# Issuing two query loads one tile ahead and splitting one read-back into three, in an offset-attention layer on eight cores

## What is computed

```
qkv = x @ qkv_w.T + qkv_b                     # q, k, v with 16 heads of 64
qs = einsum('bhnd,od->bhno', q, scale_embed)
for i, o in enumerate(OFFSETS):               # 44 offsets
    qk = einsum('bhnd,bhnd->bhn', q, shift(k, o))
    lg = qk * inv * (1.0 + qs[..., i]) + pos_bias[i]
    logits.append(where(pos >= o, lg, NEG))
p = softmax(stack(logits, -1), -1)
out = sum_i p[..., i] * shift(v, OFFSETS[i])
out = (out * if_gain) * sigmoid(x @ gate_w.T + gate_b) @ out_w.T + out_b
```

## Time and profile before

| what | us |
|---|---|
| time before, median of 2 runs | 3035.9 (3025.26 and 3046.54) |
| the profiled execution, its own time | 3036.02 |
| its span, on the slowest core (core 7) | 3033.6 |
| spans of all cores | 3019.7 to 3033.6 |
| attention, 16 tiles, in that span | 877 to 2311 |

### The profile page before, as it was taken

How to read it: one execution, slowest core, us unless ns; L and a number is a source line. 1 busy time by engine, 2 the same in 40 slices (tenths; PEclk the granted TensorE clock), 3 DMA queues, 4 the chain that set the end, 5 groups by cost and what they waited for, 6 DMA issues and landing times.

```text
span 3033.6 us, 18303 instructions; the slowest of 8 cores (3019.7 to 3033.6 us)
## 1 busy us (share of the span) xinstructions
PE 803.2 (26%) x4872; PEld 377.1 (12%) x4872; DVE 1039.1 (34%) x1142; ACT 864.1 (28%) x952; POOL 317.6 (10%) x267
## 2 busy tenths in 40 slices
PE   0139766556420111111111111111111710001620
PEld 0114322222210000000000000000000300001310
DVE  1430110000025445555454555444453043233134
ACT  1543221112123322333322333322231331003333
POOL 1000000000001011110011111011112000210000
PEclk9999998768655555555555555555555855555765
DMA  2322112223232222222222222222224032002023
GB/s 71 104 70 22 14 11 30 54 55 60 70 109 53 61 66 63 61 70 65 46 61 62 67 61 63 51 62 59 65 57 109 21 125 85 5 12 72 25 99 123
DMA packets 395686, 184.97 MB, mean 61 GB/s; under 512 B 342368, under 2 KB 353648, under 8 KB 395584
## 3 DMA queue, kind: packets, MB, share of 16 engines
q10 hardware_dynamic: 205184, 68.63, 9.8%
q1 hardware_dynamic: 147568, 82.54, 8.7%
q0 software_dynamic: 42832, 32.64, 6.2%
HBM read 111.73 MB, written 78.32 MB: 63 GB/s over the span
## 4 chain that ended last, share of the span: by engine, by line
DMA 31%; DVE 23%; ACT 16%; PE 15%; issue 7%; ACTq 5%; SPq 1%; POOL 1%; DVEq 1%; POOLq 0%
PE kqps L325 8%; DVE rbuf L538 6%; DMA rimg<-rbuf 5%; ACT rbuf L539 5%; ACTq L591 4%; DMA psp_img<-Pb 3%; DVE bandx L573 3%; DMA qtok<-qts 2%; DVE scr L570 2%; DMA accTb<-acch 2%; DMA q_img<-qtmp 2%; PE opps L754 2%; PE fps L901 2%; DMA ktok<-wcol 2%; DMA xt<-xs 2%
## 5 line engine op out<-in xcount | busy, mean ns | idle before, releaser
L523 PE MATMUL genps<-kfm,qsl 64*128 64x160 f16 (+2 forms) x768 | 92.8, 337 | 1183.6 <-DMA qtb<-qtok 691.2
L325 PE MATMUL kqps<-y1fm,wcol 128*128 128x512 f16 x1408 | 371.4, 421 | 52.5 <-ACT qtmp L367 30.3
L538 DVE CAST rbuf<-genps 128x640 f16<-128x640 f32 (+2 forms) x96 | 331.8, 3456 | 138.4 <-DMA rimg<-rbuf 111.4
L539 ACT CAST rbuf<-genps 128x640 f16<-128x640 f32 (+2 forms) x96 | 331.8, 3457 | 148.5 <-DMA psp_img<-Pb 73.2
L523 PEld LDWEIGHTS genps<-kfm,qsl 64*128 64x128 f16 x768 | 40.2, 115 | 1250.2 <-issue 1250.0
L325 PEld LDWEIGHTS kqps<-y1fm,wcol 128*128 128x128 f16 x1408 | 144.0, 106 | 235.3 <-issue 119.1
L604 ACT ACTIVATE t2b<-t2b 128x736 f32<-128x736 f32 x16 | 13.1, 816 | 547.1 <-DVE t2b L601 547.1
L664 POOL TENSOR_TENSOR acch<-vtok,Pb 128x1024 f16<-128x1024 f16 x16 | 30.3, 1892 | 1059.2 <-DMA rimg<-rbuf 800.2
L489 DVE TENSOR_TENSOR outfl<-outfl,accTb 128x128 f16<-128x128 f16 x128 | 37.6, 294 | 270.5 <-DMA psp_img<-Pb 136.1
L476 PE MATMUL pvps<-pspsb,vtok 128*64 128x128 f16 x384 | 112.2, 413 | 54.6 <-DMA band<-rimg 38.8
L358 DVE COPY vtok<-trpv 128x512 f16<-128x512 f16 x56 | 23.8, 425 | 272.5 <-PE trpv L352 272.5
(11 more groups left out here) (122 smaller groups left out, 1566.8 us busy)
## 6 DMA issues: line engine op xcount, KB each, us to landing
pspsb<-psp_img ACTq DMA_DIRECT2D x16, 1536.0 KB, 6.9
x1r<-x_img ACTq DMA_DIRECT2D x32, 512.0 KB, 3.2
xt<-xs POOLq DMA_DIRECT2D x28, 512.0 KB, 3.9
rimg<-rbuf SPq DMA_DIRECT2D x32, 416.0 KB, 2.4
rimg<-rbuf SPq DMA_DIRECT2D x32, 384.0 KB, 2.7
rimg<-rbuf SPq DMA_DIRECT2D x32, 320.0 KB, 2.2
xres<-xs ACTq DMA_DIRECT2D x16, 512.0 KB, 3.6
x_img<-x1t SPq DMA_DIRECT2D x16, 512.0 KB, 2.6
```

The lines of the kernel that those rows point to most:

```text
L325: e.matmul(_o, _s, _m, start=_st, stop=_sp),
L523: e.matmul(_o, _s, _m, start=True, stop=True, tile_position=_tp), waits, ("TS", 1))
L538: cpf = (lambda e, _o=pout, _i=pin: e.tensor_copy(_o, _i)) if eng == "vector" else \
L539: (lambda e, _o=pout, _i=pin: e.copy(_o, _i))
```

## The change

In stage A the loads of `qsl` and `pbmb` are now those of the next tile (`emit_qp_loads(qt + 1)`), with the batch name of that tile; tile 0 loads its own first. Their waits for a free buffer move with them. `qtb` is still loaded for the current tile, in a batch of its own (`"kq"`). In stage B2 the read of `psp_img` becomes three DMAs of 512 KB in one batch.

```diff
-    qsl_tok = [None, None]; pbm_tok = [None, None]
+    qsl_tok = {}; pbm_tok = {}
+
+    def emit_qp_loads(nqt):
+        if nqt >= NQT:
+            return
+        nsl = nqt % 2
+        qsl_tok[nqt] = S("scalar", lambda e, _o=qsl[nsl][:],
+                         _i=bass.AP(t["q_img"], nqt * 128, [[TOK, 128], [128 * TOK, 8], [1, 128]]):
+                         e.dma_start(out=_o, in_=_i), (last_gen.get(nqt - 2),), ("AQ", 16), batch=("ld", nqt))
+        pbm_tok[nqt] = S("scalar", lambda e, _o=pbmb[nsl][:],
+                         _i=bass.AP(t["pbm"], nqt * 128 * CW, [[CW, 128], [1, CW]]):
+                         e.dma_start(out=_o, in_=_i), (pbm_used.get(nqt - 2),), ("AQ", 16), batch=("ld", nqt))
...
     def stage_A(qt):
...
-        qsl_tok[slot] = S("scalar", lambda e, _o=qsl[slot][:],
...
-        pbm_tok[slot] = S("scalar", lambda e, _o=pbmb[slot][:],
...
+        if qt == 0:
+            emit_qp_loads(0)
+        emit_qp_loads(qt + 1)
         qtb_ev[qt] = S("scalar", lambda e, _o=qtb[:],
...
-                       (ew_lastmul.get(qt - 1),), ("AQ", 16), batch=("ld", qt))
+                       (ew_lastmul.get(qt - 1),), ("AQ", 16), batch=("kq", qt))
...
-                    waits = [qsl_tok[slot], gen_free.get((qt, genidx - 2)),
+                    waits = [qsl_tok[qt], gen_free.get((qt, genidx - 2)),
...
-               (v1, pbm_tok[slot], exp_tok.get(qt - 1)), ("VS", 1))
+               (v1, pbm_tok[qt], exp_tok.get(qt - 1)), ("VS", 1))
...
     def stage_B2(qt):
         ibase = (qt % 2) * NB * 128 * 2048
-        src = bass.AP(t["psp_img"], ibase, [[2048, 128], [128 * 2048, NB], [1, 2048]])
-        dst = bass.AP(pspsb[:].tensor, 0, [[NB * 2048, 128], [2048, NB], [1, 2048]])
-        psp_rd[qt] = S("scalar", lambda e, _o=dst, _i=src: e.dma_start(out=_o, in_=_i),
-                       (psp_wr[qt], pv_tok.get((qt - 1, 7))), ("AQ", 16), batch=("pr", qt))
+        rd = None
+        for ib in range(NB):
+            src = bass.AP(t["psp_img"], ibase + ib * 128 * 2048, [[2048, 128], [1, 2048]])
+            dst = pspsb[:, ib * 2048:(ib + 1) * 2048]
+            rd = S("scalar", lambda e, _o=dst, _i=src: e.dma_start(out=_o, in_=_i),
+                   (psp_wr[qt], pv_tok.get((qt - 1, 7))), ("AQ", 16), batch=("pr", qt))
+        psp_rd[qt] = rd
```

More of the change, by code:

```diff
@@ L494, in stage_A @@
         slot = qt % 2
-        qsl_tok[slot] = S("scalar", lambda e, _o=qsl[slot][:],
-                          _i=bass.AP(t["q_img"], qt * 128, [[TOK, 128], [128 * TOK, 8], [1, 128]]):
-                          e.dma_start(out=_o, in_=_i), (last_gen.get(qt - 2),), ("AQ", 16), batch=("ld", qt))
-        pbm_tok[slot] = S("scalar", lambda e, _o=pbmb[slot][:],
-                          _i=bass.AP(t["pbm"], qt * 128 * CW, [[CW, 128], [1, CW]]):
-                          e.dma_start(out=_o, in_=_i), (pbm_used.get(qt - 2),), ("AQ", 16), batch=("ld", qt))
+        if qt == 0:
+            emit_qp_loads(0)
+        emit_qp_loads(qt + 1)
         qtb_ev[qt] = S("scalar", lambda e, _o=qtb[:],
```

## The result

The changed kernel takes 3045.3 us (median of 29 runs) where the kernel before took 3031.3 us on the same chip (28 runs): a ratio of 1.0052, 95% interval 1.0037 to 1.0066, or 11 to 20 us more (the two medians alone are 14 us apart; here and below the interval goes with the ratio).

The account below looks back on a forecast made before the run. The prediction took each tile to be bound by the `psp_img` write of `Pb`, through the wait on SyncE's queue. Tile 0 (7.0) plus collision (5.6) added 12.6 us to 3036.0, giving 3048; range 3031 to 3062.

Parts of the forecast that it names:

- What bounds a tile: ScalarE's first copy in a tile waits for the `psp_img` write of `Pb`, 4.4 us mean; the loads have 4.1 us slack.
- The prefetch doesn't reach TensorE: Tiles 1 to 14: matmuls still wait for `qtb`, which is issued after the loads land; TensorE begins 2.6 us later.
- The cover holds, cost 0: Tiles 1 to 14: ScalarE finishes 2.6 us later, still 1.5 us before the copy released by the `psp_img` write; cost 0.
- The meeting with the write: Tiles 1 to 14: `qtb` in flight beside the large `psp_img` write delays it 0.4 us each, 5.6 us in all (0 to 13.2).
- my upper bound of 0.94: Most that `qtb` could delay the large `psp_img` write in a tile, if all of it goes first: 0.94 us.
- the mark that I had set for being wrong: The prediction counts as wrong if the large `psp_img` write takes over 5.6 us; about 5.0 was expected.
- The rule that I had left out of the sum: Engines alternate between queues, so the `psp_img` write pays for most of `qtb`: 14 x 0.8 = 11 us in place of 5.6.
- Tile 0, 7.0 us: Attention start: three loads in series without cover delay the first matmul by 7.0 us, between 5.4 and 12.3.
- The read in three, 0: Splitting the `psp_img` read into three DMAs costs 0: 13.7 us slack on ScalarE's queue, 4.5 us in tile 15.
- Rival C: Matmuls start some 4 us earlier per tile, gaining 0 in tiles 1 to 15; tile 0 pays; given 3030 us, chance 0.06.
- Rival B: First `rbuf` copy, tiles 1 to 14: cover used up, TensorE 3.8 us later; 3061 us, far end 3092; chance 0.12.
- The sum: Whole kernel: 7.0 us for tile 0 plus 5.6 for the collision of `qtb` with the write, 12.6 us slower.

Follow-up runs that it names:

- the last kernel: Changed kernel plus exact waits on SyncE's and ScalarE's queues, `qtb` in the loads' batch, stage C's matmuls waiting exactly too; against the kernel before 0.9440, 2863.5 us.

## Why the prediction was right, and where it was not

The forecast was 3048 us, 12 us over the profiled execution of before; measured were 11 to 20 us over before. Sign and size were right; the terms were less so, and that the total fits better than they do is partly luck.

- **What bounds a tile** (the write of `Pb`, by way of the wait on all of SyncE's queue): right, and shown by taking it away (0.9649), together with two other waits on the same queue. A tile became 5.9 us shorter, where ScalarE had idled 4.4 us behind the write.
- **The prefetch doesn't reach TensorE**, and `qtb` comes later: right; TensorE still waits 16 times for `qtb`. `qtb` is issued 2.7 us later (mean), as forecast, but the start slipped by 2.1 us (mean; 2.0 in the tile shown) and not 2.6, because `qtb`, issued alone, lands in 2.8 us (median) and not the 3.4 that I took from the earlier trace rows.
- **The cover holds, cost 0**: right. ScalarE's slack went to 3.2 us, not to 1.5, since the write landed later too.
- **The meeting with the write, 0.4 us in 14 tiles, 5.6 us**: the term that was mis-sized. It is 0.78 us in 13 tiles, 10.2 us. The step that failed is the reading of the low DMA share (0.42) as room: over most of the write's packets the share was already 0.66 to 0.77, and the low value came from the ends of the window. In tiles 1 to 8, where the write was hardly disturbed before, the delay is 1.04 us, even above my upper bound of 0.94, which was worked out from such shares of packet time. In tiles 9, 11 and 13 it is 0.06. In one of my 14 tiles nothing meets: in the round after tile 0, `qtb` is issued 1.5 us before the write, which lands after 4.58 us there. In this profile the write took 5.6 us and more in many tiles, the mark that I had set for being wrong; for this step I was. Nor was it so that no row could show the two together. In the kernel before, in the round after tile 12 on the slowest core, `qtb` landed 1.57 us after the write's issue, and the write took 5.83 us.
- **The rule that I had left out of the sum.** The Trainium skill, "DMA: Bandwidth & Descriptors", section "Queues, rings and completion order", says that an engine with work on several queues takes turns between them. It gives no price. With the 0.8 us of mine beside it the sum was 11 us, nearer to the 10.2 measured than my 5.6. That the load delays the write agrees with the rule; that the size fits so well is partly luck, as the mean is made of 1.04 and 0.06.
- **Tile 0, 7.0 us**: measured 7.7 by the chain of the slowest core (15.3 less 7.6) and 8.9 as the mean of the cores up to the exponential. The size was short, within its range of 5.4 to 12.3. The three landings were 4.7, 7.2 and 2.7 us, where I had 6.3, 4.5 and 3.4. The second, not the first, takes most of the weight of the key ring's loads (1.6 of the 2.1 MB moved in its time are theirs, 0.9 of 1.3 MB in the first).
- **The read in three, 0**: nothing in two comparisons speaks against it, within the 10 us or so that they can tell. Three issues take 1.3 us on ScalarE, which is idle there, and the end of the attention is still released by `accTb`.
- **Rival C** (a prefetch that reached TensorE would be worth nothing in tiles 1 to 15): borne out on the old waits as far as it was tried, with the first group of matmuls freed (0.9977, interval to 1.0006). **Rival B's** case, in which a tile pays for TensorE's later start, came true only when the cover had been taken away, at 35 us.
- **The sum**, 12.6 us, lies within the measured 11 to 20 although both terms were short (7.0 for 8.9 and 5.6 for 10.2). The terms as measured make 19.1.

## What to carry to other kernels

Idle time of an engine before an instruction is a reason to move a load only if the instruction's result is waited for; here 691 us of it hid a wait on another queue, and an earlier start of the first matmuls was worth nothing that could be seen, neither under that wait (0.9977) nor, taken alone, without it (0.9650 against 0.9649). The step to 0.9440 came when stage C's matmuls were freed as well, and the loads' part in it is open. Where a wait on a DMA means all that its queue has been given, a load issued early joins the very wait it should shorten, and each such wait that is made exact may pass the stall to the next instruction with the same kind of wait, so all of them have to be looked at. A DMA moved off its place costs where it lands: ask which transfer on the critical path it will meet, and what stands behind its issue on the same engine.

## What the runs showed that I had not expected

- A write of small pieces that uses a DMA share of 0.42 over its whole length is still delayed by 1.04 us (tiles 1 to 8) by a load of 256 KB on another queue, and by 0.48 us more by a second one. Its share while its packets move is 0.66 to 0.77.
- In the kernel before, this write lands late in tiles 9, 11 and 13 on every core: after 5.2 to 6.3 us, 5.7 in the mean of these 24, where the other 104 take 4.65. In each of the 24, and in none of the others, one packet of 16 KB that the profile calls "instruction" moves among the write's packets. For tile 9 on the slowest core, 1738 to 1744 us (queue and kind: packets, MB, share):

```profile
q1 hardware_dynamic: 4240, 0.14, 32.6%
q8 instruction: 1, 0.02, 0.9%
```

  In the last kernel, whose tiles come earlier, no such packet falls among the packets of these writes, and they take 4.7 us in the mean; in the kernel with `qtb` in the loads' batch and exact waits for them (0.9977) it falls on tiles 11 and 13, whose writes take 5.7 us, and not on tile 9, whose write takes 4.75. So the packet and the delay go together; no run moved it on purpose. Where `qtb` meets the write as well, the two delays don't add (the gap of these tiles goes from 5.76 to 5.82 us). The late writes of tiles 10, 12 and 14 on the slowest core have no such packet; in tile 12 a late `qtb` met the write, in the other two the cause is open.
- The same load lands in 2.8 us when issued alone behind a wait and in 3.4 us behind two others, 256 KB each way.
